# One core's attention and expert kernel: the first block's turn, split and first products in two parts, its inverse deviations from the variance alone, and GpSimd's remainders in another order

## The chip, the cores and the metric

The program runs on one core of one Trainium2 chip. Its time is the device time in microseconds (us) of one execution, given as the median of several runs. The engines are named as the profile names them: PE is TensorE (PEld its weight loads), DVE is VectorE, ACT is ScalarE, POOL is GpSimd, SP is SyncE, which only issues transfers here.

## The reference

Four blocks of 512 tokens with 128 features go through a layer norm. The result feeds three branches, which are added to the input: an attention over distances, a mixture of eight experts of which each token takes two, and a shared feed-forward layer.

```python
xn = (x - mean(x)) / sqrt(var(x) + 1e-5)                       # x: 4 x 512 x 128
y = xn @ U                                                     # U: 128 x 32
attn = softmax(-(n_i + n_j - 2 * y @ y.T))                     # n = sum(y * y), in each block
attention = attn @ xn

xr = xn * rsqrt(mean(xn * xn) + eps)
logits = xr @ router_w.T                                       # 8 experts, the two largest are taken
# tokens of an expert in order, at most 320 of them
routed = scatter_add(weight * ((silu(xg @ rg) * (xg @ ru)) @ rd))
shared = (silu(xn @ sg) * (xn @ su)) @ sd                      # sg, su: 128 x 1024
out = x + attention + shared + routed
```

## The kernel before

The kernel is written by hand, engine by engine: each engine has one list of instructions in a fixed order, and semaphores hold an instruction until what it needs is there. No scheduler moves anything. The 2048 tokens lie as 16 tiles of 128 (`acc`, tile `t`; four tiles make block `g`), normalized in `row1` (`xn`; the trace calls it `row`).

Every product in full precision is made of three: a number is split in a rounded part (`_hi`, made by ACT) and a remainder (`_lo`, made by DVE or POOL as the number less its rounded part), and PE multiplies hi by hi, hi by lo and lo by hi into one bank. `sw` is the shared layer's weight pair (gate and up), which comes in four quarters; `UW` holds `U` three times and the router's weights.

The beginning, on which the change works, runs like this:

- **Loads.** SP issues the first two tiles of x, then the first quarter of the shared weights, then x of blocks 1 to 3, then further weights. ACT issues the other two tiles of block 0 and after them the router's weights.
- **Statistics in two passes.** `PASSES` is block 0, then blocks 1 to 3 together. DVE makes the statistics (`stats_of`), mean and variance `mv` (`variances_of`), the variances with the two epsilons `ve`, and their reciprocals; ACT takes the root of `ve` (`root_of`); DVE makes one Newton step, which gives `rstd`, and from it `nmr` (`rstd_of`).
- **Normalizing.** `ON_DVE` and `ON_POOL` say how many tiles of a block DVE and POOL normalize; ACT takes the rest.
- **Turning.** `turn(g)` transposes the four tiles of a block on PE into one bank (`tokens_b`); ACT rounds it (`turned_hi`), DVE makes the remainder (`turned_lo`).
- **Block 0's shared layer** comes in eight chunks of 128 hidden features, six products of 512 columns each. `first_chunk` takes the first. PE's list is: warming products, the router's weights turned, `turn(0)`, ten more warming products, chunks 0 to 3, `turn(1)`, chunk 4, `turn(2)`, `project(0)`, `turn(3)`, `project(1)`, `project(2)`, chunk 5 with `project(3)` inside, the logits turned (`turn_logits`), chunks 6 and 7.
- **Routing** then runs on DVE from the turned logits on, some thirty small operations with a few other tasks among them, up to the first scores of the attention.

ACT's activation functions sit in tables that an instruction of its own loads (ACT_TABLE_LOAD in the trace). The order of ACT around the second pass is: root of pass 2, table for Silu, Silu of chunk 0, `normalize(1)`, Silu of chunk 1, `normalize(2)`. POOL's list from the first pass on is: one tile of block 0, the remainders of weight quarters 0 and 1, of `U`, then a tile each of blocks 2 and 3, quarter 3. DVE makes the remainder of quarter 2.

Of the kernel before, what the change touches and what calls it, by code (L numbers as in the profile page):

```python
# [11 lines left out]
ALU = mybir.AluOpType  # L12
ACT = mybir.ActivationFunctionType
# [6 lines left out]
P = 128  # L20
# [6 lines left out]
def moe_attention_kernel(nc, x_in, U_in, rw_in, rg_in, ru_in, rd_in, sg_in, su_in, sd_in, out):  # L27
# [23 lines left out]
    ON_DVE = [2, 3, 2, 2]  # L51
    ON_POOL = [1, 0, 1, 1]
# [70 lines left out]
    with ExitStack() as ctx:  # L123
# [58 lines left out]
        nw_a = sb("nw_a", [P, 2, NT])  # L182
        nw_b = sb("nw_b", [P, 2, NT])
        nw_c = sb("nw_c", [P, 2, NT])
        rstd = sb("rstd", [P, 2, NT])
        nmr = sb("nmr", [P, NT])
# [102 lines left out]
        tokens_b = [bank[6], bank[0], bank[3], bank[0]]  # L289
# [54 lines left out]
        ve_ready = sem("ve_ready")  # L344
        root_ready = sem("root_ready")
        rstd_ready, nmr_ready = sem("rstd_ready"), sem("nmr_ready")
# [21 lines left out]
        sw_hi_s, sw_ready, sw_ready_dve = sem("sw_hi_s"), sem("sw_ready"), sem("sw_ready_dve")  # L368
# [28 lines left out]
        def _(sp):  # L397
# [45 lines left out]
            sp.wait_ge(sw_ready, CS // 2 - 1)  # L443
            sp.wait_ge(sw_ready_dve, 1)
# [60 lines left out]
        def _(pool):  # L505
# [53 lines left out]
            pool.wait_ge(rstd_ready, len(PASSES))  # L559
# [4 lines left out]
            pool.wait_ge(sw_ready_dve, 1)  # L564
# [92 lines left out]
        def _(act):  # L657
            C = nc.scalar

            def root_of(gs):  # L660
                ts = slice(TG * gs[0], TG * (gs[-1] + 1))
                act.wait_ge(ve_ready, pass_of[gs[0]] + 1)
                C.activation(root[:, :, ts], ve[:, :, ts], ACT.Sqrt, scale=0.25).then_inc(root_ready, 1)
# [9 lines left out]
            def turned_hi(g):  # L673

                act.wait_ge(xnT_turned, g + 1)
                C.copy(xnT_hi[:, S * g:S * g + S], tokens_b[g][:, :]).then_inc(xnT_hi_s, 1)

# [114 lines left out]
            act.wait_ge(rw_turned, 1)  # L792
            C.copy(rw_hi, rw_ps).then_inc(rw_hi_s, 1)
# [90 lines left out]
        def _(dve):  # L884
# [15 lines left out]

            V.memset(fill[:, 0:1], 0.0)
# [13 lines left out]
            def stats_of(g):  # L915

                dve.wait_ge(x_in_s[g], 16)
                for t in range(TG * g, TG * g + TG):
# [3 lines left out]
                mark(last)  # L922

# [693 lines left out]
```

## Time and profile before

| | |
|---|---|
| median of 3 runs | 156.39 us (156.25 to 156.74) |
| the profiled execution | 156.25 us, of which the span of the trace is 154.5 us |
| PE busy | 149.5 us, 97% of the span |
| DVE, ACT, POOL busy | 122.4, 109.6 and 86.7 us |
| granted TensorE clock | 1.00 in every slice |

The page gives each engine's busy time first. A share of 97% for PE says that PE had work in its pipe nearly always, the warming products among it; it does not say which wait a change can move. For that the chain of work that ended last is read, which goes back from the last instruction to what released it, and then the instructions in order of time, engine by engine, with the idle time before each and what ended it. All times of a trace count from the start of its span.

### The profile page before, as it was taken

What the parts mean: (1) busy time and instruction counts of PE and PEld (TensorE: products, weight loads), DVE (VectorE), ACT (ScalarE), POOL (GpSimd) and SP (SyncE); (2) the same over time, 40 slices, a digit from 0 to 9 for tenths busy, and PEclk for the clock granted to TensorE, in tenths of its full rate; (3) what the DMA queues carried; (4) which work ended last, traced back from release to release, by engine and by line L of the source; (5) the groups of instructions that cost most, each with busy time, mean ns of one, the idle gap of its engine ahead of it and who ended that gap; (6) DMA issues with size and microseconds to landing.
All of it is one profiled execution on the core that took longest, in us unless ns stands there. A gap on an engine that the chain in (4) does not pass through costs nothing.

```text
span 154.5 us, 3092 instructions
## 1 busy us (share of the span) xinstructions
PE 149.5 (97%) x925; PEld 132.6 (86%) x925; DVE 122.4 (79%) x299; ACT 109.6 (71%) x227; POOL 86.7 (56%) x111
## 2 busy tenths in 40 slices
PE   6999999999999999999999999999999999999992
PEld 6878777888998878998888899999999998788891
DVE  3999969999827999877999677877877866778973
ACT  3369999999495987656964797996875663645860
POOL 7653432767777788777744063689878373460000
PEclk9999999999999999999999999999999999999999
DMA  4999999991110077442239605212321010175562
GB/s 133 300 265 122 185 301 349 339 285 53 52 53 6 8 220 208 122 127 78 68 80 300 196 2 192 63 34 66 100 77 30 28 36 25 30 242 139 204 199 75
DMA packets 26879, 20.82 MB, mean 135 GB/s; under 512 B 2383, under 2 KB 23077, under 8 KB 26864
## 3 DMA queue, kind: packets, MB, share of 16 engines
q1 hardware_dynamic: 24784, 17.86, 43.1%
q0 software_dynamic: 1792, 2.65, 5.4%
q8 instruction: 7, 0.11, 0.3%
q10 hardware_dynamic: 288, 0.14, 0.3%
q14 instruction: 8, 0.07, 0.1%
HBM read 12.46 MB, written 7.92 MB: 132 GB/s over the span
## 4 chain that ended last, share of the span: by engine, by line
PE 84%; DVE 8%; DMA 2%; ACT 1%; issue 1%; POOL 1%; DVEq 0%
PE bank L1259 8%; PE bank L1261 8%; PE bank L1260 8%; PE bank L1388 7%; PE bank L1385 7%; PE bank L1382 7%; PE bank L1344 7%; PE bank L1483 7%; PE bank L1484 7%; PE bank L1485 7%; PE bank L1501 3%; PE bank L1329 2%; DMA acc<-in_L_attn_x_dram 2%; PE bank L1513 1%; PE bank L1357 1%
## 5 line engine op out<-in xcount | busy, mean ns | idle before, releaser
L731 ACT ACTIVATE silu<-bank 128x512 f32<-128x512 f32 (+1 forms) x64 | 33.3, 520 | 27.3 <-PE bank L1388 26.8
L1079 DVE TENSOR_TENSOR bank<-bank,silu 128x320 f32<-128x320 f32 (+1 forms) x56 | 32.7, 584 | 18.4 <-ACT silu L731 11.7
L621 POOL DMA_INDIRECT slots_dram<-row,slot_i x32 | 34.9, 1092 | 10.3 <-issue 9.4
L640 POOL DMA_INDIRECT routed_dram<-eo,xg x24 | 23.3, 970 | 15.5 <-DVE eo L1120 9.9
L1085 DVE TENSOR_TENSOR hid_lo<-bank,hid_hi 128x320 fp32r<-128x320 f32 (+1 forms) x56 | 31.7, 565 | 0.0
L739 ACT CAST hid_hi<-bank 128x320 fp32r<-128x320 f32 (+1 forms) x56 | 27.5, 492 | 0.4 <-DVE bank L1079 0.4
L1382 PE MATMUL bank<-xnT_hi,sw_hi 128*128 128x512 f32 x31 | 13.0, 419 | 0.0
L628 POOL TENSOR_TENSOR ew_lo<-sw_raw,ew_hi 128x1024 fp32r<-128x1024 f32 x3 | 7.2, 2404 | 9.7 <-ACT ew_hi L755 9.7
L1388 PE MATMUL bank<-xnT_hi,sw_lo 128*128 128x512 f32 x31 | 12.3, 398 | 0.0
L1259 PE MATMUL bank<-xnT_hi,sw_hi 128*128 128x512 f32 x31 | 12.3, 397 | 0.0
L1385 PE MATMUL bank<-xnT_lo,sw_hi 128*128 128x512 f32 x31 | 12.3, 396 | 0.0
L1260 PE MATMUL bank<-xnT_lo,sw_hi 128*128 128x512 f32 x31 | 12.2, 395 | 0.0
L1261 PE MATMUL bank<-xnT_hi,sw_lo 128*128 128x512 f32 x31 | 12.2, 395 | 0.0
L1483 PE MATMUL bank<-hid_hi,yL 128*128 128x512 f32 (+1 forms) x32 | 12.0, 376 | 0.0
L1484 PE MATMUL bank<-hid_lo,yL 128*128 128x512 f32 (+1 forms) x32 | 11.9, 372 | 0.0
L1485 PE MATMUL bank<-hid_hi,yR 128*128 128x512 f32 (+1 forms) x32 | 11.9, 372 | 0.0
L1344 PEld LDWEIGHTS bank<-row,probs 128*128 128x128 f32 x96 | 11.0, 192 | 0.2
L1344 PE MATMUL bank<-row,probs 128*128 128x129 f32 x96 | 11.0, 275 | 0.0
L1382 PE MATMUL bank<-xgT_hi,ew_hi 128*128 128x320 f32 x24 | 8.1, 336 | 0.0
L723 ACT ACTIVATE probs<-bank 128x512 f32<-128x512 f32 x12 | 6.2, 617 | 2.2 <-PE bank L1329 2.2
L755 ACT CAST ew_hi<-sw_raw 128x512 fp32r<-128x512 f32 x12 | 7.5, 633 | 0.3 <-DMA sw_raw<-in_L_ffn_ru_dram 0.3
L1442 PEld LDWEIGHTS bank<-sd,hid_s 128*128 128x128 f32 x64 | 7.5, 192 | 0.2
(228 smaller groups left out, 387.1 us busy)
## 6 DMA issues: line engine op xcount, KB each, us to landing
sw_raw<-in_L_ffn_rg_dram SPq DMA_DIRECT2D x8, 256.0 KB, 3.0
sw_raw<-in_L_ffn_ru_dram SPq DMA_DIRECT2D x8, 256.0 KB, 3.4
rd_raw<-in_L_ffn_rd_dram SPq DMA_DIRECT2D x8, 256.0 KB, 4.0
routed_dram<-fill SPq DMA_DIRECT2D x1, 2048.0 KB, 11.5
routed<-routed_dram SPq DMA_DIRECT2D x8, 256.0 KB, 4.0
slots_dram<-fill SPq DMA_DIRECT2D x1, 1300.0 KB, 12.3
xg<-slots_dram SPq DMA_DIRECT2D x8, 130.0 KB, 2.7
row<-row SPq DMA_DIRECT2D x1, 1024.0 KB, 8.0
```

Of the source, the lines that this page charges most:

```text
L621: G.indirect_dma_start(slots_dram, bass.IndirectOffsetOnAxis(slot_i[:, k, t:t + 1], 0), row[:, t, 0:RW], None, bounds_check=E * CAP - 1, o ...
L640: G.indirect_dma_start(routed_dram, bass.IndirectOffsetOnAxis(xg[0:n, e % XB, r, 1:2].bitcast(I32), 0), eo[0:n, e % 2, r, :], None, bounds ...
L731: C.activation(silu[:, q % 2, 0:n], gate_bank(q)[:, 0:n], ACT.Silu).then_inc(silu_ready, 1)
L739: C.copy(hid_hi[:, w % PARTS, 0:n], up_bank(q)[:, 0:n]).then_inc(hid_hi_s, 1)
L1079: V.tensor_tensor(hid, up[:, 0:n], silu[:, q % 2, 0:n], ALU.mult).then_inc(hid_ready, 1)
L1085: V.tensor_tensor(hid_lo[:, w % PARTS, 0:n], up_bank(q)[:, 0:n], hid_hi[:, w % PARTS, 0:n].bitcast(F32), ALU.subtract).then_inc(hid_split, 1)
L1259: M(o, w_hi, m_hi, start=True, stop=False)
L1260: M(o, w_hi, m_lo, start=False, stop=False)
L1261: return M(o, w_lo, m_hi, start=False, stop=True)
L1344: last = M(down_b[h][:, (D + 1) * (i % 2):(D + 1) * (i % 2 + 1)], probs_of(b)[:, j, P * i:P * i + P], xn_ones[:, TG * b + j, :], start=(j ...
L1382: M(gate, w_hi(0), m_hi, start=True, stop=False)
L1385: M(gate, w_hi(0), m_lo, start=False, stop=False)
```

## The change

For block 0 the normalized tiles are turned, rounded and split in two halves of two tiles (256 columns). `turn_first` turns the first two as soon as DVE has normalized them (`first_pair`), in bank 6, and the other two in bank 7; `first_turned_hi` and `first_turned_lo` make the parts by halves, and `first_chunk` makes its six products once for each half, so twelve of 256 columns. DVE now normalizes three tiles of block 0 and ACT one, POOL none.

ACT's root reads the variance `mv` directly, with the epsilon as a bias (`quarter_eps`), and no longer waits for `ve`. In pass 1 only the layer norm's deviation is made, in pass 2 the router's for all 16 tiles, so pass 2 has a second root on ACT. A root of a dummy (`warm_root`) stands ahead. ACT issues the router's weights before its two tiles of x. The rounding of weight quarter 0 stands before ACT's normalizing.

POOL waits for `nmr` of pass 1 before the remainders of quarters 0 and 1, and for `nmr` of pass 2 before that of quarter 2, which DVE made before. In `project` the order of the three products is hi by hi, lo by hi, hi by lo, and only the last waits for the remainder of the tokens; the chunks of block 0 wait for a weight's remainder only at the product that uses it. PE's warming is 40 products before the router's turn and 15 after it.

```diff
-    ON_DVE = [2, 3, 2, 2]
-    ON_POOL = [1, 0, 1, 1]
+    ON_DVE = [3, 3, 2, 2]
+    ON_POOL = [0, 0, 1, 1]
...
-            normalize(0)
+            pool.wait_ge(nmr_ready, 1)
             split_shared(0)
             split_shared(1)
+            pool.wait_ge(nmr_ready, len(PASSES))
+            split_shared(2)
             pool.wait_ge(U_hi_s, 1)
...
-            pool.wait_ge(sw_ready_dve, 1)
             normalize(2)
             normalize(3)
...
-                act.wait_ge(ve_ready, pass_of[gs[0]] + 1)
-                C.activation(root[:, :, ts], ve[:, :, ts], ACT.Sqrt, scale=0.25).then_inc(root_ready, 1)
+                act.wait_ge(mv_ready, pass_of[gs[0]] + 1)
+                last = C.activation(root[:, 0, ts], mv[:, ts, 1], ACT.Sqrt, scale=0.25, bias=quarter_eps[:, 0:1])
+                if gs is PASSES[-1]:
+                    last = C.activation(root[:, 1, :], mv[:, :, 1], ACT.Sqrt, scale=0.25 * (1.0 + RMS_EPS),
+                                        bias=quarter_eps[:, 1:2])
+                last.then_inc(root_ready, 1)
...
+            def first_turned_hi(h):
+
+                cols = slice(2 * P * h, 2 * P * (h + 1))
+                act.wait_ge(first_turned, h + 1)
+                C.copy(xnT_hi[:, cols], first_tokens_b[h][:, 0:2 * P]).then_inc(xnT_hi_s, 1)
...
+            act.dma_start(rw_raw[:, :], rw_in).then_inc(rw_loaded, 16)
             act.dma_start(acc[:, 2:TG, :], x_v[0][:, 2:TG, :]).then_inc(x_second_half, 16)
-            act.dma_start(rw_raw[:, :], rw_in).then_inc(rw_loaded, 16)
+            act.wait_ge(eps_set, 1)
+            C.activation(warm_root[:, :], quarter_eps[:, :], ACT.Sqrt)
             root_of(PASSES[0])
+            round_shared(0)
             normalize(0)
-            round_shared(0)
-            turned_hi(0)
+            first_turned_hi(0)
+            first_turned_hi(1)
             round_shared(1)
...
+                last.then_inc(mv_ready, 1)
+                dve.wait_ge(mv_ready, pass_of[gs[0]] + 1)
+                last = V.tensor_scalar(ve[:, 0, ts], mv[:, ts, 1], LN_EPS, None, ALU.add)
+                if gs is PASSES[-1]:
+                    last = V.tensor_scalar(ve[:, 1, :], mv[:, :, 1], 1.0 + RMS_EPS, LN_EPS * RMS_EPS, ALU.mult, ALU.add)
                 then(last)
-                V.tensor_scalar(ve[:, 0, ts], mv[:, ts, 1], LN_EPS, None, ALU.add)
-                V.tensor_scalar(ve[:, 1, ts], mv[:, ts, 1], 1.0 + RMS_EPS, LN_EPS * RMS_EPS, ALU.mult, ALU.add
-                                ).then_inc(ve_ready, 1)
-                dve.wait_ge(ve_ready, pass_of[gs[0]] + 1)
-                mark(V.reciprocal(nw_a[:, :, ts], ve[:, :, ts]))
+                fs = flat_of(gs)
+                mark(V.reciprocal(nw_a[:, fs], ve_flat[:, fs]))
...
+            def first_turned_lo(h):
+                cols = slice(2 * P * h, 2 * P * (h + 1))
+                dve.wait_ge(xnT_hi_s, h + 1)
+                V.tensor_tensor(xnT_lo[:, cols], first_tokens_b[h][:, 0:2 * P], xnT_hi[:, cols].bitcast(F32),
+                                ALU.subtract).then_inc((first_lo, xnT_ready)[h], 1)
...
-            stats_of(1)
+            stats_of(1, range(2))
+            first_turned_lo(0)
+            first_turned_lo(1)
+            stats_of(1, range(2, TG))
             stats_of(2)
-            turned_lo(0)
             stats_of(3)
             variances_of(PASSES[1])
             split_router()
             rstd_of(PASSES[1])
             normalize(1)
             mult_chunk(0)
-            third = slice(4 * P, 6 * P)
-            dve.wait_ge(sw_hi_s, 3)
-            V.tensor_tensor(sw_lo[:, :, third], sw_raw[:, :, third], sw_hi[:, :, third].bitcast(F32), ALU.subtract
-                            ).then_inc(sw_ready_dve, 1)
...
+            def turn_first():
+                for h in range(2):
+                    if h == 0:
+                        pe.wait_ge(first_pair, 1)
+                    else:
+                        pe.wait_ge(xn_ready, 1)
+                        pe.wait_ge(xn_ready_act, 1)
+                    for j in range(2 * h, 2 * h + 2):
+                        last = nc.tensor.transpose(first_tokens_b[h][:, P * (j % 2):P * (j % 2) + P], xn[:, j, :],
+                                                   ident[:, :])
+                    last.then_inc(first_turned, 1)
...
-                pe.wait_ge(xnT_ready, g + 1)
+                pe.wait_ge(xnT_hi_s, g + 2)
                 if g == 0:
                     pe.wait_ge(silu_ready, 3)
                 elif g == 1:
                     pe.wait_ge(silu_ready, 4)
                 else:
                     pe.wait_ge(hid_ready, g + 1)
-                parts(y_b[g][0:3 * R + E, :], UW_hi[:, :], UW_lo[:, :], xnT_hi[:, cols], xnT_lo[:, cols]
-                      ).then_inc(y_done, 1)
+                y = y_b[g][0:3 * R + E, :]
+                M(y, UW_hi[:, :], xnT_hi[:, cols], start=True, stop=False)
+                M(y, UW_lo[:, :], xnT_hi[:, cols], start=False, stop=False)
+                pe.wait_ge(xnT_ready, g + 1)
+                M(y, UW_hi[:, :], xnT_lo[:, cols], start=False, stop=True).then_inc(y_done, 1)
...
-                m_hi, m_lo = xnT_hi[:, 0:S], xnT_lo[:, 0:S]
-                gate, up = gate_bank(0)[:, :], up_bank(0)[:, :]
                 pe.wait_ge(sw_hi_s, 1)
-                pe.wait_ge(xnT_hi_s, 1)
-                M(gate, w_hi[:, 0, :], m_hi, start=True, stop=False)
-                M(up, w_hi[:, 1, :], m_hi, start=True, stop=False)
-                pe.wait_ge(sw_ready, 1)
-                M(gate, w_lo[:, 0, :], m_hi, start=False, stop=False)
-                M(up, w_lo[:, 1, :], m_hi, start=False, stop=False)
-                pe.wait_ge(xnT_ready, 1)
-                M(gate, w_hi[:, 0, :], m_lo, start=False, stop=True).then_inc(gate_done, 1)
-                M(up, w_hi[:, 1, :], m_lo, start=False, stop=True).then_inc(chunk_done, 1)
+                for h in range(2):
+                    cols = slice(2 * P * h, 2 * P * (h + 1))
+                    m_hi, m_lo = xnT_hi[:, cols], xnT_lo[:, cols]
+                    gate, up = gate_bank(0)[:, cols], up_bank(0)[:, cols]
+                    pe.wait_ge(xnT_hi_s, h + 1)
+                    M(gate, w_hi[:, 0, :], m_hi, start=True, stop=False)
+                    M(up, w_hi[:, 1, :], m_hi, start=True, stop=False)
+                    pe.wait_ge(sw_ready, 1)
+                    M(gate, w_lo[:, 0, :], m_hi, start=False, stop=False)
+                    M(up, w_lo[:, 1, :], m_hi, start=False, stop=False)
+                    pe.wait_ge((first_lo, xnT_ready)[h], 1)
+                    gate_last = M(gate, w_hi[:, 0, :], m_lo, start=False, stop=True)
+                    up_last = M(up, w_hi[:, 1, :], m_lo, start=False, stop=True)
+                    if h == 1:
+                        gate_last.then_inc(gate_done, 1)
+                        up_last.then_inc(chunk_done, 1)
...
-            warm(WARMING)
+            warm(2 * WARMING // 3)
             pe.wait_ge(consts, 1)
             pe.wait_ge(rw_loaded, 16)
             nc.tensor.transpose(rw_ps, rw_raw[:, :], ident[0:E, 0:E]).then_inc(rw_turned, 1)
-            turn(0)
-            warm(10)
+            warm(WARMING // 4)
+            turn_first()
             first_chunk()
             up_of_block(0, 1)
             up_of_block(0, 2)
```

In `up_of_block` (not shown) only the waits change, as said above.

ACT's list from the start of the program to the first tokens rounded, before:

```order
L781 DMA acc<-in_L_attn_x_dram 128x2x128
L782 DMA rw_raw<-in_L_ffn_router_w_dram 8x128
L663 ACT_TABLE_LOAD
L663 ACTIVATE root<-ve 128x2x4
L669 ACTIVATE row<-acc,nmr,rstd 128x128
L779 CAST sw_hi<-sw_raw 128x2x256
L676 CAST xnT_hi<-bank 128x512
```

and now:

```order
L795 DMA rw_raw<-in_L_ffn_router_w_dram 8x128
L796 DMA acc<-in_L_attn_x_dram 128x2x128
L798 ACT_TABLE_LOAD
L798 ACTIVATE warm_root<-quarter_eps 128x2
L667 ACTIVATE root<-mv,quarter_eps 128x4
L793 CAST sw_hi<-sw_raw 128x2x256
L677 ACTIVATE row<-acc,nmr,rstd 128x128
L690 CAST xnT_hi<-bank 128x256 x2
```

The two tiles of x went behind the router's weights, and the root reads `mv` where it read `ve`.

DVE's list from the first pass's last small product to the second pass's variances, before (`row` is written by the normalizing, `xnT_lo` is the tokens' remainder):

```order
L952 SCALAR_TENSOR_TENSOR nmr<-mv,rstd 128x4
L958 TENSOR_SCALAR row<-acc,mv,rstd 128x128 x2
L921 BN_STATS stats<-acc 128x6 x8
L965 TENSOR_TENSOR xnT_lo<-bank,xnT_hi 128x512
L921 BN_STATS stats<-acc 128x6 x4
L928 BN_AGGR mv<-stats 128x2 x12
```

and now:

```order
L979 SCALAR_TENSOR_TENSOR nmr<-mv,rstd 128x4
L985 TENSOR_SCALAR row<-acc,mv,rstd 128x128 x3
L941 BN_STATS stats<-acc 128x6 x2
L1001 TENSOR_TENSOR xnT_lo<-bank,xnT_hi 128x256 x2
L941 BN_STATS stats<-acc 128x6 x10
L952 BN_AGGR mv<-stats 128x2 x12
```

A third tile is normalized there, and the remainder of the tokens, now in two pieces, stands behind two statistics where it stood behind eight.

POOL's list after its constants, before:

```order
L552 TENSOR_SCALAR row<-acc,mv,rstd 128x128
L546 TENSOR_TENSOR sw_lo<-sw_raw,sw_hi 128x2x256 x2
L561 TENSOR_TENSOR UW_lo<-U_raw,UW_hi 128x32 x3
L552 TENSOR_SCALAR row<-acc,mv,rstd 128x128 x2
L567 TENSOR_TENSOR std<-ve,rstd 128x16
```

and now:

```order
L550 TENSOR_TENSOR sw_lo<-sw_raw,sw_hi 128x2x256 x3
L566 TENSOR_TENSOR UW_lo<-U_raw,UW_hi 128x32 x3
L556 TENSOR_SCALAR row<-acc,mv,rstd 128x128 x2
L571 TENSOR_TENSOR std<-ve,rstd 128x16
```

The tile of block 0 is gone, and the third `sw_lo` stands between the second and `UW_lo`, ahead of the tiles of blocks 2 and 3.

## Rows read from the trace of the kernel before

**Rows 1.** Chain of work that ended last, 0 to 24 us: start, length, what

```profile
6.22 0.89 POOL row L552
7.24 0.64 PE bank L1279 x4
...
8.64 0.47 PE bank L1418
...
21.60 0.45 PE bank L1288 x4
```

**Rows 2.** PE in order of time, around turn(1) and project(3): start, length, instruction

```profile
14.34 0.60 PE L1279 MATMUL bank<-ident,row 128*128 128x128 f32 x4
...
18.89 0.39 PE L1261 MATMUL bank<-xnT_hi,UW_lo 128*104 128x512 f32 x1
19.12 0.40 PE L1382 MATMUL bank<-xnT_hi,sw_hi 128*128 128x512 f32 x1
19.48 0.48 PE L1259 MATMUL bank<-xnT_hi,UW_hi 128*104 128x512 f32 x1
```

**Rows 3.** ACT in order of time, 0 to 14 us; in brackets the idle time before

```profile
0.79 0.48 ACTq L781 DMA_DIRECT2D acc<-in_L_attn_x_dram  x1
1.30 0.63 ACTq L782 DMA_DIRECT2D rw_raw<-in_L_ffn_router_w_dram  x1
1.96 1.28 ACT L663 ACT_TABLE_LOAD   x1 [1.96 <-issue]
...
7.91 0.59 ACT L676 CAST xnT_hi<-bank 128x512 fp32r<-128x512 f32 x1 [0.57 <-PE bank L1279]
...
9.07 0.46 ACT L790 CAST UW_hi<-U_raw 128x32 fp32r<-128x32 f32 x3
...
11.25 0.22 ACT L663 ACTIVATE root<-ve 128x24 f32<-128x24 f32 x1 [1.15 <-DVE ve L931]
11.49 1.28 ACT L731 ACT_TABLE_LOAD   x1
...
13.28 0.48 ACT L669 ACTIVATE row<-acc,nmr,rstd 128x128 f32<-128x128 f32 x1
```

**Rows 4.** DMA issues, 0.7 to 1.9 us: size, median us from issue to landing

```profile
acc<-in_L_attn_x_dram ACTq DMA_DIRECT2D x1, 128.0 KB, 2.9
sw_raw<-in_L_ffn_sg_dram SPq DMA_DIRECT2D x1, 128.0 KB, 2.5
...
sw_raw<-in_L_ffn_su_dram SPq DMA_DIRECT2D x1, 128.0 KB, 3.5
```

**Rows 5.** DVE in order of time, 3 to 13 us

```profile
3.46 0.87 DVE L921 BATCH_NORM_STATS2 stats<-acc 128x6 f32<-128x128 f32 x4 [1.52 <-DMA acc<-in_L_attn_x_dram]
...
4.78 0.40 DVE L930 TENSOR_SCALAR ve<-mv 128x4 f32<-128x4 f32 x1
...
6.22 0.60 DVE L958 TENSOR_SCALAR row<-acc,mv,rstd 128x128 f32<-128x128 f32 x2
...
8.53 0.69 DVE L965 TENSOR_TENSOR xnT_lo<-bank,xnT_hi 128x512 fp32r<-128x512 f32 x1 [0.15 <-ACT xnT_hi L676]
...
10.97 0.17 DVE L930 TENSOR_SCALAR ve<-mv 128x12 f32<-128x12 f32 x1
...
12.40 0.87 DVE L958 TENSOR_SCALAR row<-acc,mv,rstd 128x128 f32<-128x128 f32 x3
```

**Rows 6.** Groups of instructions by shape: busy us, mean ns of one, idle before

```profile
L739 ACT CAST hid_hi<-bank 128x320 fp32r<-128x320 f32 x32 | 13.5, 423 | 0.0
L1102 DVE TENSOR_TENSOR xgT_lo<-bank,xgT_hi 128x320 fp32r<-128x320 f32 x8 | 3.9, 482 | 0.2
```

**Rows 7.** POOL in order of time, 4 to 14 us

```profile
4.63 0.53 POOL L541 MEMSET lgT<- 128x512 f32 x1
...
7.42 1.27 POOL L546 TENSOR_TENSOR sw_lo<-sw_raw,sw_hi 128x512 fp32r<-128x512 f32 x1 [0.33 <-ACT sw_hi L779]
...
12.43 0.71 POOL L561 TENSOR_TENSOR UW_lo<-U_raw,UW_hi 128x32 fp32r<-128x32 f32 x3 [1.88 <-DVE rstd L949]
```

More of the change, by code:

```diff
@@ L181, in moe_attention_kernel @@
         root = sb("root", [P, 2, NT])
-        nw_a = sb("nw_a", [P, 2, NT])
-        nw_b = sb("nw_b", [P, 2, NT])
-        nw_c = sb("nw_c", [P, 2, NT])
+        nw_a = sb("nw_a", [P, 2 * NT])
+        nw_b = sb("nw_b", [P, 2 * NT])
+        nw_c = sb("nw_c", [P, 2 * NT])
         rstd = sb("rstd", [P, 2, NT])
+        quarter_eps = sb("quarter_eps", [P, 2])
+        warm_root = sb("warm_root", [P, 2])
+        ve_flat, root_flat, rstd_flat = [t[:, :, :].rearrange("p k t -> p (k t)") for t in (ve, root, rstd)]
         nmr = sb("nmr", [P, NT])
@@ L792, in _ @@
             act.wait_ge(rw_turned, 1)
+            act.wait_ge(xnT_ready, 1)
             C.copy(rw_hi, rw_ps).then_inc(rw_hi_s, 1)
@@ L899, in then @@
                 settle()
+            V.memset(quarter_eps[:, 0:1], 0.25 * LN_EPS)
+            V.memset(quarter_eps[:, 1:2], 0.25 * LN_EPS * RMS_EPS).then_inc(eps_set, 1)
             V.memset(fill[:, 0:1], 0.0)
@@ L913, in _, with stats_of @@
             V.tensor_copy(slot0[:, :, :], slot0_i[:, :, :]).then_inc(slot0_set, 1)
-            def stats_of(g):
+            def stats_of(g, own=range(TG)):
                 dve.wait_ge(x_in_s[g], 16)
-                for t in range(TG * g, TG * g + TG):
+                for t in range(TG * g + own.start, TG * g + own.stop):
                     if t == 2:
@@ L922, in stats_of, with flat_of @@
                 mark(last)
+            def flat_of(gs):
+                return slice(0, TG) if gs is PASSES[0] else slice(TG, 2 * NT)
             def variances_of(gs):
@@ L945, in rstd_of @@
                 settle()
-                then(V.tensor_tensor(nw_b[:, :, ts], nw_a[:, :, ts], root[:, :, ts], ALU.mult))
-                then(V.scalar_tensor_tensor(out=nw_c[:, :, ts], in0=nw_b[:, :, ts], scalar=-4.0,
-                                            in1=root[:, :, ts], op0=ALU.mult, op1=ALU.mult))
-                V.scalar_tensor_tensor(out=rstd[:, :, ts], in0=nw_c[:, :, ts], scalar=3.0, in1=nw_b[:, :, ts],
+                fs = flat_of(gs)
+                then(V.tensor_tensor(nw_b[:, fs], nw_a[:, fs], root_flat[:, fs], ALU.mult))
+                then(V.scalar_tensor_tensor(out=nw_c[:, fs], in0=nw_b[:, fs], scalar=-4.0,
+                                            in1=root_flat[:, fs], op0=ALU.mult, op1=ALU.mult))
+                V.scalar_tensor_tensor(out=rstd_flat[:, fs], in0=nw_c[:, fs], scalar=3.0, in1=nw_b[:, fs],
                                        op0=ALU.add, op1=ALU.mult).then_inc(rstd_ready, 1)
@@ L959, in normalize @@
                                            ALU.subtract, ALU.mult)
+                    if t == 1:
+                        last.then_inc(first_pair, 1)
                 last.then_inc(xn_ready, 1)
```

24 lines of the change are left out of this document (11 added, 13 removed).

## The prediction

> **What bounds the kernel now.** I read the chain that ended last first, since PE is busy nearly throughout and its share alone tells nothing. At the beginning the chain runs from x over small operations on DVE and one tile on POOL to PE's first products at 8.64 us, then over PE alone to the turned logits at 21.60, and from there into the routing on DVE [rows 1]. So whatever moves those logits moves the rest: behind them I find no wait with slack that could give back or swallow some tenths. The question is not when the first product starts, but when the logits are turned.
>
> Second, PE between the two. Products of 512 columns follow each other every 0.23 us (18.89 to 19.12). There is one stall: 19.12 to 19.48, and the product behind it takes 0.48 instead of 0.40; together 0.13 + 0.08 = 0.21 us lost at project(3) [rows 2]. Third, who feeds PE. `turn(1)`, at 14.34 [rows 2], needs ACT's tile of block 1, which runs 13.28 to 13.76 [rows 3]. A handover to a transpose takes 0.13 us (7.11 to 7.24) [rows 1], so it could begin at 13.89: the slack is 0.45 us. That tile stands on ACT behind the root of pass 2 (11.25), a table load of 1.28 and a Silu [rows 3], and the root behind DVE's second pass of statistics. So the second thing to read is what the change does to DVE ahead of that pass.
>
> **The change, part by part.**
>
> *The table ahead: nothing.* The load already starts at 1.96 and is over at 3.24 [rows 3], long before the first `ve` at 4.78 [rows 5]. The dummy root lies in ACT's idle time.
>
> *The order of ACT's transfers: a loss.* The third statistic needs ACT's two tiles. Four statistics take 0.87, so one starts every 0.2, the third at 3.87, without a wait [rows 5]. The transfer, issued at 0.79, now stands behind the router's weights, whose issue takes 0.48 (as the first on this queue did) to 0.63, so it is issued at 1.30 to 1.45, middle 1.37 [rows 3]. From issue to landing it took 2.9; SP's weight transfers of the same size, issued at 1.3 and 1.8, between which it now falls, took 2.5 and 3.5 [rows 4]. Lower end: 1.30 + 2.5 = 3.80, no wait. Upper end: 1.45 + 3.5 = 4.95. I take the middle of 2.9 (its own row) and 3.5, as it now shares its time with those weights: 1.37 + 3.2 = 4.57. The third statistic then starts at 4.59, 0.72 late.
>
> *The root from the variance: a gain of 0.23.* Two operations on `ve` become one. The first took 0.40, while POOL's memset ran to 5.16 [rows 7]; pass 2's, with POOL idle, took 0.17 [rows 5]. The root runs beside `ve` and the reciprocal. Normalizing block 0 starts at 6.22 + 0.72 - 0.23 = 6.71.
>
> *Halves.* Two tiles take 0.60 on DVE [rows 5], so the first pair is there at 7.31; the tile on POOL took 0.89 [rows 1]. Add 0.13 for the handover, 0.43 for two transposes (four take 0.64 with the last one's drain [rows 1]; between 0.32 and 0.64), 0.03 to ACT, and rounding 256 columns: 512 take 0.59 [rows 3], 320 take 0.42 [rows 6], so 0.37. That is 8.27, and 0.14 later, as before, the first product: 8.41 instead of 8.64, a gain of 0.23. Twelve products of half the width take at least the six's 6 x 0.23 = 1.4, at most twice that, if each needs a full step; I take 1.5. PE comes to `turn(1)` at about 14.2 (8.41 + 5.70, the old distance, + 0.1).
>
> *DVE ahead of pass 2: a loss.* The start is 0.49 late. The third tile adds 0.27 (three take 0.87, two 0.60 [rows 5]). Its two statistics end 1.25 after the start of normalizing, at 7.96, and the remainder waits for ACT until 8.30: 0.34 of idle instead of 0.15, so +0.19. Two remainders of half the width cost 0.06 more than one (512: 0.69 [rows 5]; 320: 0.48 [rows 6]; so 0.41 each, less 0.08 of overlap). Sum: 0.49 + 0.27 + 0.19 + 0.06 = 1.01. The variances of pass 2 come 1.01 us later.
>
> *ACT behind it.* The root may now start with `ve` (10.97 [rows 5]) instead of behind it (11.25): -0.28. A second root is added: +0.12, the further cost of one small operation in a row of three that take 0.46 [rows 3]. ACT's tile comes 1.01 - 0.28 + 0.12 = 0.85 later, and with 0.45 of slack `turn(1)` begins 0.40 later, at 14.74. PE, there at 14.2, waits half a microsecond: the earlier first products are lost here, and twice the width's cost in them would still lie mostly in this wait.
>
> *POOL and `project`.* The remainder of quarter 2 moves from DVE, where it stood behind the part that counts, to POOL ahead of its tiles: 1.27, then 0.71 for `U` [rows 7] and 0.89 for a tile. It begins with pass 2's `nmr`, some 12.4 + 1.01 + 0.1 = 13.5, and the tile of block 2 is done at 16.4, 16.5 at PE. `turn(2)` comes one turn and six products after `turn(1)`, at 16.5 to 16.6: covered, but with nothing to spare; each tenth that POOL is late costs a tenth. In `project(3)` the remainder is needed 0.47 later than now, so the stall of 0.21 goes. POOL's wait for the first `nmr` holds only remainders that are not needed before 8.7 and are done by 8.2.
>
> *Sum:* the logits come 0.40 - 0.21 = 0.19 later. The profiled execution took 156.25, its sum would be 156.44; it was the fastest of three whose median is 156.39, and on that I forecast 156.39 + 0.19 = 156.58, about 156.6.
>
> **The rivals.** *x comes in time.* If the two tiles land at 3.8 after all, the 0.72 goes, all else stands, and the time is 156.39 + 0.19 - 0.72 = 155.86. For it: the landing of 2.5 of a neighbour [rows 4], and the first half of x, which now has the transfer engines to itself. Against it: two weight transfers are issued around it. It decides once x lands before 3.93.
>
> *x lands as late as the weights (slower).* If its packets alternate with those of both weight transfers, it lands with the second, at 1.80 + 3.5 = 5.3: 0.73 more than I took, 157.31. For it: 3.5 against 2.5 for two equal transfers half a microsecond apart [rows 4]. Against it: it would be half done before the second starts. It decides from 4.85 on. The Trainium skill, "DMA: Bandwidth & Descriptors", section "Issuing engines are not separate DMA queues", says that transfers from different engines run on the same 16 DMA engines and interleave; no row here shows two queues with these sizes against each other.
>
> *POOL holds DVE (slower).* POOL's first remainder now starts beside DVE's normalizing of block 0, about 6.9, and runs 1.27. If DVE had to wait for its end at 8.17, its second tile would start 1.2 late, and the end with it: 157.8. For it: `ve` started at 4.78 and ended with POOL's memset, 0.40 instead of 0.17 [rows 5, 7]. Against it: three tiles on DVE took their usual 0.87 beside POOL's remainders of `U` [rows 5, 7], and two took 0.60 beside POOL's own tile [rows 1, 5]. The Trainium skill, "SBUF — State Buffer", section "SBUF: two separate sides", states it as a rule: an exclusive lock on a shared pair of ports, by which one of the two fully blocks the other. The memset's row agrees, the rows of normalizing do not, and the measurement decides.
>
> **How the numbers follow.** The forecast, with x landing between 3.93 and 4.85: 0.53. x in time: 0.20. x with the weights: 0.20. POOL holding DVE: 0.05. POOL so late at `turn(2)` that over 0.3 is added: 0.02. About 0.3%, 0.47 us, is what a measurement of this kernel can tell from no change; the first case lies within it (156.39 - 0.45 to 156.39 + 0.47), the second is faster, the others slower: 0.20, 0.53, 0.27. The range reaches to 155.8, just beyond the early case, and to 157.2, into the late one, which leaves out its upper half and POOL's.
>
> **What would show it.** The third statistic at 4.6, and normalizing at 6.7. First product at 8.4, of 256 columns. Pass 2's variances at 11.9, ACT's tile of block 1 at 14.1, and in front of `turn(1)` a wait of PE of half a microsecond for ACT, where there was none. No stall at project(3), the turned logits at 21.8. I am wrong if x is there before 4, if PE does not wait at `turn(1)`, or if DVE's tiles of block 0 take over 0.4 each.

## The result

The changed kernel takes 157.89 us (157.62 to 158.73, 6 runs), the kernel before, beside it, 156.51 (156.25 to 156.76): a ratio of 1.010, 95% interval 1.0083 to 1.0118, so about 1.5 us slower. The forecast was 156.6 with a range to 157.2. The price is that of the rival which had been given the smallest weight but one, POOL holding DVE, at 157.8. The runs below show that this mechanism is at work. That the number agrees so well is partly luck: that rival had the hold at 1.2 us, it is 0.96, and half a microsecond of the loss is there without any hold, where the forecast had 0.19. Other terms of the forecast were wrong, a later start of normalizing that the profile does not show and two gains that did not come, and cancelled each other only in part.

### The profile page after: what moved, and what is told of

Same layout as the page of the kernel before. It is cut to its first block, busy times and chain, and to the rows that moved or that the text cites. A ratio compares the mean times of both kernels' runs of the same rounds, so it can differ in the third digit from the quotient of the medians.

```text
span 155.9 us, 3073 instructions
## 1 busy us (share of the span) xinstructions
PE 149.2 (96%) x916; PEld 132.1 (85%) x916; DVE 123.9 (79%) x301; ACT 110.1 (71%) x230; POOL 86.9 (56%) x111
## 4 chain that ended last, share of the span: by engine, by line
PE 76%; DVE 10%; ACT 8%; issue 2%; DMA 2%; ACTq 0%; DVEq 0%
PE bank L1430 7%; PE bank L1392 7%; PE bank L1433 7%; PE bank L1436 7%; PE bank L1294 7%; PE bank L1293 7%; PE bank L1292 7%; PE bank L1534 7%; PE bank L1536 7%; PE bank L1535 7%; PE bank L1552 3%; PE bank L1377 2%; DVE row L985 2%; DMA acc<-in_L_attn_x_dram 2%; DVE stats L941 2%
## 5 line engine op out<-in xcount | busy, mean ns | idle before, releaser
L1114 DVE TENSOR_TENSOR bank<-bank,silu 128x320 f32<-128x320 f32 (+1 forms) x56 | 32.8, 585 | 18.4 <-ACT silu L745 11.7
L644 POOL DMA_INDIRECT routed_dram<-eo,xg x24 | 23.3, 969 | 15.5 <-DVE eo L1155 9.9
L550 POOL TENSOR_TENSOR sw_lo<-sw_raw,sw_hi 128x512 fp32r<-128x512 f32 x4 | 5.2, 1301 | 9.0 <-ACT sw_hi L793 4.6
```

Of the source, the lines that this page charges most:

```text
L644: G.indirect_dma_start(routed_dram, bass.IndirectOffsetOnAxis(xg[0:n, e % XB, r, 1:2].bitcast(I32), 0), eo[0:n, e % 2, r, :], None, bounds ...
L1114: V.tensor_tensor(hid, up[:, 0:n], silu[:, q % 2, 0:n], ALU.mult).then_inc(hid_ready, 1)
```

## The profile after

DVE in order of time (start, length, instruction, count; in brackets the idle time before):

```profile
4.13 0.49 DVE L941 BATCH_NORM_STATS2 stats<-acc 128x6 f32<-128x128 f32 x2 [0.56 <-DMA acc<-in_L_attn_x_dram]
...
5.06 0.17 DVE L955 TENSOR_SCALAR ve<-mv 128x4 f32<-128x4 f32 x1
...
6.23 1.81 DVE L985 TENSOR_SCALAR row<-acc,mv,rstd 128x128 f32<-128x128 f32 x3
...
8.71 0.76 DVE L1001 TENSOR_TENSOR xnT_lo<-bank,xnT_hi 128x256 fp32r<-128x256 f32 x2 [0.28 <-ACT xnT_hi L690]
9.39 2.02 DVE L941 BATCH_NORM_STATS2 stats<-acc 128x6 f32<-128x128 f32 x10
...
12.38 0.17 DVE L955 TENSOR_SCALAR ve<-mv 128x12 f32<-128x12 f32 x1
...
13.86 1.81 DVE L985 TENSOR_SCALAR row<-acc,mv,rstd 128x128 f32<-128x128 f32 x3
```

x's third tile was there for a statistic at 4.13, not 4.59, and normalizing starts at 6.23, where it started before (6.22, [rows 5]). But three tiles take 1.81 us in both blocks, where three took 0.87 [rows 5]. POOL beside them, and DVE's tiles one by one (duration in ns: least, median, most), first those of block 0, then those of block 1:

```profile
6.40 1.30 POOL L550 TENSOR_TENSOR sw_lo<-sw_raw,sw_hi 128x512 fp32r<-128x512 f32 x1 [1.20 <-DVE nmr L979]
...
14.02 1.31 POOL L550 TENSOR_TENSOR sw_lo<-sw_raw,sw_hi 128x512 fp32r<-128x512 f32 x1 [3.17 <-DVE nmr L979]
```
```profile
L985 DVE TENSOR_SCALAR row<-acc,mv,rstd x3: 336/343/1293, 6.2 to 7.7; 128x128 f32<-128x128 f32 x3
L985 DVE TENSOR_SCALAR row<-acc,mv,rstd x3: 334/342/1305, 13.9 to 15.3; 128x128 f32<-128x128 f32 x3
```

One tile of each three takes 1.3 us, the others the usual 0.34. It is the second, which begins just after POOL's remainder and ends 0.09 behind it. PE pays at both places:

```profile
8.82 0.36 PE L1468 MATMUL bank<-xnT_hi,sw_hi 128*128 128x256 f32 x1 [0.30 <-ACT xnT_hi L690]
...
15.72 0.66 PE L1324 MATMUL bank<-ident,row 128*128 128x128 f32 x4 [1.02 <-DVE row L985]
```

The first product comes at 8.82 (8.64 before [rows 1]), and at `turn(1)` PE waits 1.02 us, for DVE and not for ACT. From there the chain that ended last runs on like this (start, length, what):

```profile
13.86 1.02 DVE row L985 x2
...
15.34 0.34 DVE row L985
...
15.72 0.66 PE bank L1324 x4
...
18.52 0.59 ACT xnT_hi L684
...
20.26 0.52 ACT sw_hi L793
...
29.24 0.59 ACT norm_parts L716
...
29.85 0.76 DVE norm_parts L1086
```

This is not the path that I had read. It does not go over the turned logits (22.93 here) and the routing, but from `turn(2)` over ACT, which works nearly without a gap (10.97 of 11.31 us) to the last of its rounded norms, and DVE's operation on these. That operation is a good marker. In the kernel before it stands at 28.35:

```profile
28.35 0.76 DVE L1051 SCALAR_TENSOR_TENSOR norm_parts<-norm_parts,minus_lo,bank 16x512 fp32r<-16x512 f32 x1
```

From it to the end of the span it is 126.1 us before and 126.0 after; of the 19 kernels profiled here 17 have 126.0 to 126.2. So the 1.50 us by which it is late are the loss, and they can be divided: block 0's normalizing 0.01 later, from there to block 1's normalizing 7.63 instead of 6.18 (+1.45), from there to the marker 15.99 instead of 15.95.

## Experiments

Ratios are to the kernel before, run beside on the same chip, with 95% intervals.

### Does POOL's remainder hold DVE's tiles?

The theory: a remainder of POOL keeps DVE's `tensor_scalar` tiles waiting until it ends. The rival: the loss lies in the order of the transfers, or in the halves themselves. The first edit lets POOL's first remainder start when DVE's tiles are done:

```diff
-            pool.wait_ge(nmr_ready, 1)
+            pool.wait_ge(xn_ready, 1)
             split_shared(0)
```

> The changed kernel with one wait moved: POOL's remainders of weight quarters 0 and 1 wait until DVE's three tiles of block 0 are done, not until the first pass's nmr. Theory (POOL's remainder, an operation with two inputs from SBUF, holds DVE's tile until it ends): the second tile of block 0 takes 0.34 instead of 1.29, the variances of pass 2 come 0.94 earlier (12.35 to 11.4), and as the second collision, in block 1, stays and moves along, turn(1) comes 0.94 earlier: 157.89 - 0.94 = 156.95. Rival (the long tile is only a mark of the later x and of DVE's fuller list): no change within 0.3, about 157.8.

Measured: 156.9, ratio 1.0040 (1.0028 to 1.0052), as expected. The tiles, block 0 and block 1:

```profile
L985 DVE TENSOR_SCALAR row<-acc,mv,rstd x3: 341/344/345, 6.3 to 6.8; 128x128 f32<-128x128 f32 x3
L985 DVE TENSOR_SCALAR row<-acc,mv,rstd x3: 334/342/1314, 12.9 to 14.4; 128x128 f32<-128x128 f32 x3
```

The hold of block 0 is gone and that of block 1, which was not touched, is still there. From block 0's normalizing to block 1's it is 6.67 instead of 7.63: 0.96, and the time fell by 0.9. Now both (`pool.wait_ge(xn_ready, 2)` ahead of `split_shared(2)` as well):

> As the kernel with the first wait moved, and POOL's remainder of quarter 2 also waits, until DVE's three tiles of block 1 are done. Theory (POOL holds DVE): no DVE tile takes over 0.45; turn(1) now follows ACT's tile at about 14.4 (15.72 in the changed kernel), but POOL's tile of block 2 comes behind a remainder (1.3) and U (0.7) that start at 13.85, so turn(2) waits for POOL until 16.85 (17.89 in the changed kernel): 157.89 - 1.04 = 156.85. If POOL were not late at turn(2): 156.5. Rival (work moved onto DVE, not the collision, costs the time): not below 157.5.

Measured: 156.84, ratio 1.0034 (1.0022 to 1.0047), as expected. All six tiles take 0.34, and against the run before it gains next to nothing: POOL's remainder now stands beside DVE's first tiles of block 2 (two take 0.97 instead of 0.60), POOL's own tile behind it, and PE waits 0.49 at `turn(2)`. Quarter 2's remainder back on DVE, as in the kernel before, and the first left where the change put it:

> The changed kernel with quarter 2's remainder back on DVE, as in the kernel before; GpSimd's first remainder still starts with the first nmr. Holding theory (DVE's second tile waits for the end of GpSimd's remainder): block 0's three tiles stay at 1.81 us, block 1's fall from 1.81 to 0.87. The end follows only as far as turn(1) does: ACT's tile, done at 15.18 in the changed kernel, then sets it, so turn(1) comes at 15.3 instead of 15.72, and the time is 157.8 - 0.4 = 157.4. If the second hold cost its full 0.94, 156.9; if it cost nothing, 157.8.

Measured: 157.94, ratio 1.0089 (1.0069 to 1.0108); block 1's tiles take 0.87 again, and against the changed kernel it gains 0.2, less than the intervals are wide. The expectation counted the hold, but not that DVE gets 0.60 of work back (the remainder's step): from block 1's normalizing to the marker it is 15.91 instead of 15.99. The opposite, the kernel before with only this remainder moved to POOL:

> The kernel before with quarter 2's remainder moved to GpSimd, from pass 2's nmr on, as in the changed kernel; nothing else. Holding theory: GpSimd's remainder starts at 12.5 and ends at 13.8, DVE's second tile of block 1 takes 1.3 and ends at 13.9, the third at 14.2, and turn(1), which stood at 14.34 behind PE's products, can begin at 14.3: the hold is there in full, three tiles 1.8 instead of 0.87, and costs nothing, 156.3 to 156.6. If a hold of 0.94 always costs its length, 157.3.

Its tiles of block 1, one by one:

```profile
L957 DVE TENSOR_SCALAR row<-acc,mv,rstd x3: 336/342/1326, 12.9 to 14.4; 128x128 f32<-128x128 f32 x3
```

Measured: 156.48, ratio 1.001 (1.000 to 1.002). The hold is there in full and costs 0.15 us (0 to 0.3). DVE saves the remainder, and in the profile PE does not wait at `turn(1)`. (In this profile PE and DVE are both half a microsecond late ahead of it, since PE's warming products lasted until 7.63, where the kernel before had them done at 6.81, and the first product came at 9.14.)

How long does a hold last? The remainders in four pieces of 128 elements each (`for k in range(4)` over 64 columns, the signal on the last):

> The changed kernel with each of GpSimd's remainders of the shared weights cut into four operations of 128 elements (about 0.45 us each by 0.25 for 32 elements and 1.29 for 512), starting where it did. If a hold lasts as long as the one operation that GpSimd is in, DVE's second tile ends about 0.09 behind the first piece's end, at about 0.5 instead of 1.29 us, and three tiles take 0.9 to 1.3; the time falls to 156.6 to 157.0, as GpSimd's tiles come some 0.4 later. If the hold lasts while GpSimd has work in its queue, the three tiles take more than 1.8 and the time is 158 or above.

DVE's tiles of block 0, and POOL's pieces beside them:

```profile
L988 DVE TENSOR_SCALAR row<-acc,mv,rstd x3: 342/480/495, 6.6 to 7.3; 128x128 f32<-128x128 f32 x3
L552 POOL TENSOR_TENSOR sw_lo<-sw_raw,sw_hi x4: 450/451/487, 6.8 to 8.0; 128x128 fp32r<-128x128 f32 x4
```

Measured: 157.36, ratio 1.0050 (1.0034 to 1.0066), less gained than expected. Why is not shown; in its profile x came for 4.50 instead of 4.13. But the durations decide: 0.48 and 0.50 instead of 1.29, and three tiles 1.15. A hold lasts as long as the one operation, and between two of POOL's operations DVE gets in. That is why the rows that spoke against this rival misled: POOL's remainders of `U` take 0.71 for three [rows 7], some 0.25 each, which is less than a tile's own 0.34. DVE's tiles of block 1 beside them, in the kernel before:

```profile
L958 DVE TENSOR_SCALAR row<-acc,mv,rstd x3: 334/336/362, 12.4 to 12.9; 128x128 f32<-128x128 f32 x3
```

The longest, 0.362, is the first, and it ends 0.08 behind the first of POOL's three pieces, as the held tiles do. In the twelve profiles with these pieces beside this tile it takes 0.354 to 0.364, in the other seven 0.342 to 0.345. So the hold was in the rows, with 0.02 us to be seen of it.

Does it need two inputs? The remainder replaced by a product with zero, of one input and the same size (so the shared weights' remainder adds nothing in this run):

> The changed kernel with POOL's remainders of the four quarters of the shared weights replaced by an operation of the same size with one input (the raw weights times zero), so the remainder's products add nothing: a part of the computation is left out. It tells what in POOL's operation holds DVE. If two inputs from SBUF are needed: DVE's second tiles take 0.34, and the time falls to about 156.5, by 0.94 for block 0 and some 0.4 for block 1. If any operation of POOL holds DVE's tile: the second tiles take as long as POOL's operation lasts, and the time stays above 157.5 unless that operation is much shorter than 1.3.

DVE's tiles of block 0, and POOL's operation beside them:

```profile
L984 DVE TENSOR_SCALAR row<-acc,mv,rstd x3: 334/344/636, 6.7 to 7.5; 128x128 f32<-128x128 f32 x3
L550 POOL TENSOR_SCALAR sw_lo<-sw_raw x1: 1545/1545/1545, 6.8 to 6.8; 128x512 fp32r<-128x512 f32 x1
```

Measured: 156.70, ratio 1.0022 (1.0008 to 1.0036), between the two expectations: the operation of 1.55 us holds one tile for 0.3 and lets the next one through while it is still running. With one input the hold is short, not absent; why, no run here shows.

### x's order, and a memset that had hidden it

> The changed kernel with ACT's two transfers in the old order, the two tiles of x ahead of the router's weights. In the changed kernel x landed at 4.11, and the third statistic waited until 4.13 where it stood at 3.87 before. If that wait lies on the path in full: 157.89 - 0.26 = 157.63, both collisions stay (two tiles of DVE at 1.3). If the order cost what I had taken: 157.2. If it is swallowed by a later wait: 157.9.

The two `dma_start` lines of ACT exchanged. Measured: 157.16, ratio 1.0053 (1.0028 to 1.0077), at its second expectation, 0.7 less than the changed kernel by the ratios. Normalizing began at 5.66, and both holds were in place. The same edit the other way, in the kernel before:

> The kernel before with x's two tiles issued on ACT's queue behind the router's weights, nothing else. In seven profiles of kernels with this order the third statistic started at 4.13 to 4.72, mean 4.38; in three with x first at 3.54 to 3.87, mean 3.66. Nothing behind it has slack of that size up to the turned logits, so the whole 0.7 should reach the end: 157.0 to 157.2. If only the 0.26 counts by which the changed kernel's profile was later than the one of before, 156.7; if other work hides it, 156.4.

DVE's statistics of the third and fourth tile:

```profile
4.69 0.49 DVE L921 BATCH_NORM_STATS2 stats<-acc 128x6 f32<-128x128 f32 x2 [1.13 <-DMA acc<-in_L_attn_x_dram]
```

Measured: 156.74, ratio 1.0025 (1.0014 to 1.0036): 0.4, half of what was expected. In the eight profiles with x second the third statistic starts at 4.13 to 4.72, in the eleven with x first at 3.54 to 4.02, 0.63 apart on average, so the delay of 0.72 in the forecast was of the right size. What it missed is that the kernel before, with x as early as in its profile, did not profit from it: its first `ve` starts at 4.78 and ends at 5.18, 0.02 behind POOL's memset of `lgT` [rows 5, 7]. (Of the profiles with x first and the memset in its place, `ve` was done before the memset began, at 4.69, only in the two with x for 3.54 and 3.58; there normalizing started at 5.65 and 5.66.) With that memset behind POOL's tile, and nothing else changed:

```diff
-            G.memset(lgT[:, :], 0.0).then_inc(lgT_zeroed, 1)
...
             normalize(0)
+            G.memset(lgT[:, :], 0.0).then_inc(lgT_zeroed, 1)
             split_shared(0)
```

> The kernel before with GpSimd's memset of lgT moved behind its tile of block 0, nothing else. If that memset holds DVE's first ve operation (0.40 instead of 0.17, ending 0.02 behind it), normalizing of block 0 starts at 5.9 to 6.0 instead of 6.22, DVE, ACT and PE all come 0.25 earlier, the norms of ACT too (27.4 instead of 27.7), and the time is 0.2 to 0.3 less: 156.1 beside 156.4 of before. If the operation was slow for another reason, normalizing stays at 6.2 and the time at 156.4.

DVE's first operation on `ve`:

```profile
4.94 0.17 DVE L930 TENSOR_SCALAR ve<-mv 128x4 f32<-128x4 f32 x1
```

Measured: 156.11, ratio 0.9981 (0.9967 to 0.9995). `ve` takes 0.17, and it is faster than the kernel before by 0.3. (In the one profiled execution x came late, 4.02, so its normalizing starts at 6.21; the gain is in the times.)

### What sets the end

`project`'s new order of products alone, in the kernel before:

> The kernel before with project's products in the changed kernel's order (the remainder of the activations last, waited for there), nothing else. The stall of 0.21 at project(3) should go and the turned logits come at 21.2 instead of 21.4: 0.2 less, 156.2 beside 156.4 of the kernel before. If the stall's place is taken by another wait, no difference.

Measured: 156.39, ratio 0.9999 (0.9988 to 1.0010). The stall is gone and the turned logits come at 21.22 instead of 21.43, but the marker stands at 28.32 instead of 28.35, since ACT's norms are not earlier. With the memset moved as well:

> As the run before, with project's products in the changed kernel's order as well. If ACT's work from turn(3) to the norms sets the end as soon as the logits come early, the second edit adds nothing to the first: 156.1. If only the logits set it, both add up: 155.9.

Measured: 156.19, ratio 0.9983 (0.9967 to 0.9998), the same as the memset alone. Earlier logits gain nothing. In its profile normalizing starts at 5.79, but PE was at its warming products until 7.39 and the first product came at 8.90, so the marker stands at 28.54; in the run before it stands at 28.41, and in the kernel before at 28.35. How the memset's gain reaches the end is therefore in neither profile; it is shown by the times alone. Now the changed kernel without holds, first with x second, then with x first:

> As the run before, and GpSimd's first remainder starts only after DVE's tiles of block 0, so that neither remainder runs beside DVE's tiles. Holding theory: both blocks' three tiles 0.87; turn(1) at about 14.5 (ACT's tile sets it, as with both remainders after the tiles), turn(2) no longer late for GpSimd's own tile, 16.3 instead of 17.0; the time 156.2 to 156.3, the kernel before's. If something else in the change costs what is left, it stays at 156.8.

> As the run before, with x's two tiles issued ahead of the router's weights again. Normalizing at 5.7 instead of 6.3 (it was 5.66 with this order alone), first product at 7.3, held 0.1 to 0.2 by GpSimd's first remainder, ACT's tile and turn(1) half a microsecond earlier, at 13.9: 155.6 to 155.8, below the kernel before's 156.25. If the order of the two transfers costs only what its own run showed between medians (0.6 to 0.7), 155.6; if the early start is lost behind ACT's tile, 156.2.

Measured: 156.99, ratio 1.0031 (1.0020 to 1.0042), and 156.63, ratio 1.0009 (0.9997 to 1.0020), both 0.7 to 1.0 above what was expected. Without holds the order of x's transfers is worth 0.3 us (1.0031 against 1.0009). In the second run, PE and DVE:

```profile
14.08 0.63 PE L1329 MATMUL bank<-ident,row 128*128 128x128 f32 x4 [0.51 <-ACT row L678]
```
```profile
7.52 0.76 DVE L1002 TENSOR_TENSOR xnT_lo<-bank,xnT_hi 128x256 fp32r<-128x256 f32 x2 [0.62 <-ACT xnT_hi L691]
...
28.57 0.76 DVE L1087 SCALAR_TENSOR_TENSOR norm_parts<-norm_parts,minus_lo,bank 16x512 fp32r<-16x512 f32 x1 [0.27 <-ACT norm_parts L717]
```

`turn(1)` is 0.26 earlier than before (14.34 [rows 2]), the marker 0.22 later. What is also later, by 0.26, is DVE's normalizing of block 1 (12.66 against 12.40 [rows 5]). It is that, and not `turn(1)`, with which the end goes: it stands 15.8 to 16.1 ahead of the marker in 16 of 19 profiles, 15.5 and 15.7 in the two where DVE neither makes quarter 2's remainder nor is held for long, and 18.4 in the last run of this section. The chain that ended last shows the way:

```profile
1.40 4.35 PE bank L1304 x40
5.91 0.94 PE bank L1304 x15
7.11 0.38 ACT xnT_hi L691
...
11.71 1.28 ACT L746
13.00 0.61 ACT silu L746
...
27.96 0.59 ACT norm_parts L717
```

It begins with PE's warming products (`L1304`), goes over DVE's pass 2 to ACT's roots, the load of Silu's table and the first Silu, and from there over DVE and ACT to the norms. DVE's stretch between the two normalizings had become longer, 7.01 instead of 6.18, and 0.62 of it is a wait for ACT's first rounded half. Half of this wait comes from the warming: the first two tiles were done at 6.25, but PE began to turn them at 6.69, behind its warming products. Where PE was free (the run of ratio 1.0040) the wait is 0.29 and the stretch 6.67. Is it the third tile that makes it longer than 6.18?

> The changed kernel with x first, quarter 2's remainder on DVE, and the third tile of block 0 back on GpSimd ahead of its first remainder (so no remainder stands beside DVE's tiles). Against the run with x first and no holds DVE's pass ahead of block 1 loses one tile, 0.26: normalizing of block 1 7.0 - 0.26 = 6.75 behind that of block 0, ACT's norms at 27.7 instead of 27.96, the time 0.25 less, 156.2 to 156.4 beside 156.4 of before. If the third tile was not on the path, 156.6.

> As the run before, with 7 instead of 15 warming products of PE after the router's turn. With x first the first tiles are there at 6.25 and PE began to turn them at 6.7, behind its warming. The first products come 0.3 earlier, DVE waits less for the first rounded half, and DVE, ACT and PE come up to 0.3 earlier: 155.9 to 156.1. If the granted clock falls for want of the warming, the first products take twice as long and the time is above 157.

Measured: 156.65, ratio 1.0011 (0.9997 to 1.0025), and 156.57, ratio 1.0002 (0.9990 to 1.0014), both above what was expected. The third tile is not the cost: without it DVE waits 0.54 for ACT's half, with it 0.29 (in the run of ratio 1.0040), and the stretch is 6.67 in both, so it stands in a wait. The shorter warming is not tested by its run: in the profile the memset held `ve`, normalizing began at 6.22, and PE was through with its warming at 5.87, before there was a tile to turn. Next the wait was filled, with the memset out of the way:

```diff
-            stats_of(1, range(2))
+            stats_of(1)
             first_turned_lo(0)
             first_turned_lo(1)
-            stats_of(1, range(2, TG))
```

> As the last run with the tile on GpSimd and the short warming, and DVE takes all four statistics of block 1 ahead of the halves' remainders instead of two, and GpSimd's memset of lgT stands behind its first remainder. If DVE's wait for ACT's first half (0.54) is what the halves cost, it falls to 0.2 or less and the stretch from block 0's normalizing to block 1's from 6.68 to about 6.3; with the memset out of the way normalizing of block 0 at 5.7 to 6.0 instead of 6.22. Together 0.4 to 0.6: 156.0 to 156.2 beside 156.4 of before, as with the memset moved alone (156.1), so that the halves add nothing to it. If the halves pay once they cost DVE nothing, 155.8 or less; if the wait was not the cause, 156.4 and more.

Measured: 156.04, ratio 0.9967 (0.9953 to 0.9981), as expected, and faster than both kernels. In its profile the wait is 0.37 and the stretch 6.55, less of a fall than I had expected. PE was late again, behind its warming:

```profile
5.96 1.05 PE L1301 MATMUL bank<-ones_bf 128*128 128x128 bf16 x10
```

The first two tiles were done at 6.53, and PE turned them from 6.85 on. Whether the run is faster than the memset alone these intervals do not tell, so a gain from the halves is not shown. Nor is it shown how much the wait for ACT's half costs, and what a shorter warming gains when x is early stays untested.

One run lost much. In the kernel of ratio 1.0009, ACT's tile of block 1 was put ahead of the first Silu, and quarter 2's remainder ahead of DVE's product with that Silu:

> The run without holds and with x first, and in it ACT makes its tile of block 1 ahead of the first Silu, and DVE quarter 2's remainder ahead of the first product with that Silu. There PE waited 0.51 for ACT's tile at turn(1), and turn(2), at 16.23, for GpSimd's tile, which stands behind quarter 2's remainder. Now ACT's tile is done at 13.5 and GpSimd's at 15.1: turn(1) at 13.6 instead of 14.08, turn(2) at 15.5 instead of 16.23, the time 0.5 to 0.7 less, 155.8 to 156.1 beside 156.4 of before. If the later Silu holds the next chunk's products instead, no gain, 156.6.

ACT in order of time:

```profile
13.35 0.50 ACT L678 ACTIVATE row<-acc,nmr,rstd 128x128 f32<-128x128 f32 x1 [1.09 <-DVE nmr L980]
13.87 1.28 ACT L746 ACT_TABLE_LOAD   x1
15.16 1.08 ACT L746 ACTIVATE silu<-bank 128x512 f32<-128x512 f32 x2
```

Measured: 158.53, ratio 1.013 (1.0083 to 1.0177), far above both expectations. The table of Silu is loaded where its first user stands. Behind the root it had filled ACT's wait for `nmr`; now ACT waits first (1.09) and loads then, PE stands for 1.74 us, and the granted clock, 1.00 until then, is 0.65 on average from 16 to 20 us, most of it at the lower of its two levels, 1.2 GHz.

## Why the prediction was wrong, point by point

- **Table ahead, first products, their widths: right.** The load runs at 1.87, in idle time. From the start of normalizing to the first product it is 1.65 without a hold (forecast 1.70), and twelve half products take 1.53 (forecast 1.5; 1.82 to 1.92 in the five runs whose first product comes at 1.65, where PE then stands before the weights' remainder).
- **x 0.72 late, less 0.23 for the root: the size right, the place wrong.** The delay is 0.63 on average over all profiles, 0.26 in this one. But the kernel before had its own hold at that point, and the forecast saw it (the first `ve` ended with the memset) without drawing the conclusion that its early x gained nothing there. So normalizing starts as before in this profile. By the ratios the order costs 0.7 us with the holds and 0.3 without.
- **DVE's pass, +0.52 without the start: right as a sum, but its parts are not prices.** From normalizing to pass 2's `ve` it is 5.20 without a hold, 4.75 before [rows 5]: +0.45. The third tile, the longer wait (0.29, forecast 0.34) and the halves are in it about as forecast. But without the third tile the wait grows by as much, so taking it away gains nothing.
- **ACT's roots: half right.** The first starts with `ve` (12.38), as said; from its start to the table load it is 0.53 instead of 0.24 [rows 3], so the second root costs 0.29 and not 0.12, which eats the 0.28 that the earlier start gains.
- **"POOL holds DVE", chance 0.05: this is the step that failed.** In the sum it stood at nothing. The hold is real, 0.96 us at block 0, which is two thirds of the loss. "The rows of normalizing do not" agree, I wrote, and let them decide, but these rows were of other operations: pieces so short that 0.02 of a hold shows, and one of a single input. The Trainium skill, "SBUF — State Buffer", section "SBUF: two separate sides", says that the one which comes first holds the ports for its whole instruction. For a remainder of two inputs that starts ahead of the tile the runs agree, at 1.3 and at 0.45 us; for one input of 1.55 us they do not, as it held for 0.3 only.
- **POOL's remainder of quarter 2: not "covered".** It was priced by when it is done, not by what stands beside it. Its hold lasts 0.94 and costs nearly nothing, because DVE was rid of 0.60 of work and, as I read it, waits of others lay beside it.
- **0.45 of slack at `turn(1)`: wrong.** PE does have it, but the end does not hang on PE there; it goes with DVE's pass ahead of block 1 and ACT behind it, and that path has no slack that the runs show. So even without a hold the forecast was 0.3 too low: with x second and no hold the ratio is 1.0031, half a microsecond, of which the order of x's transfers is 0.3.
- **The stall at project(3), -0.21: it went, and gained nothing.** "Behind them I find no wait with slack that could give back or swallow some tenths" was wrong for gains: a second path, ACT's norms, is as long to within 0.1 us.

## What to carry to other kernels

Where two engines can hold each other, ask of every moved operation what will run beside it, and compare only with rows of the same operation, the same inputs and the same length: beside an operation shorter than the neighbour's own time a hold hardly shows (0.02 us here). Before pricing a slack, look for a second path of the same length; here a marker behind both, at a constant distance from the end, told more than PE's waits did. And when a step starts at the same time although its input came earlier, something else holds it: in this kernel moving one memset gained 0.3 us. And before an edit is called useless, see in its profile that it could act: the shorter warming was tried in a run in which something else held the start.

## What the runs showed of the hardware that I had not expected

- Only DVE's `tensor_scalar` operations (tiles, `ve`) were seen held. DVE's statistics took 0.28 each beside a remainder of POOL, and a reciprocal 0.18 beside the memset.
- Behind an operation of POOL with two inputs a held tile ends 0.08 to 0.09 later, a held `ve` 0.02 to 0.03 behind the memset.
- An operation of POOL with one input holds a tile for a part of its length only.
- The same transfer, issued at 1.42 to 1.43 behind the router's weights, was there for a statistic at 4.13 to 4.72 in eight kernels, one profile of each.
- PE's warming products follow each other every 0.11 us at first and every 0.06 later, and when that changes differs from profile to profile, with 1.00 as the granted clock throughout: the same 60 products ended between 6.13 and 7.63 in the six kernels that have them. In the two where they ended last, at 7.39 and 7.63, the first product came at 8.90 and 9.14 instead of 8.64. So one profile can differ from another by half a microsecond in a place that no edit touched.
